# Five kinds of POOL work moved to ACT, DVE, transfers and a sum from PSUM, in a fused attention and routed transformer block with hand-written order lists

## The chip, the cores and the metric

The kernel runs on one core of a Trainium2 chip. The metric is the device time of one execution in microseconds (us), median of the runs shown; lower is better. A core has TensorE (PE, with its weight loads shown apart as PEld), VectorE (DVE), ScalarE (ACT), GpSimd (POOL) and SyncE (SP), which here issues every transfer. Each engine runs its own instructions in the order in which they were written and waits on semaphores.

## The reference, cut to what matters

Sixteen sequences of 512 tokens of width 128 go through two sublayers, each with a residual and a layer norm. All data are float32.

```python
# first sublayer: causal attention, 16 heads of 8
q, k, v = heads(x @ w_q.T), heads(x @ w_k.T), heads(x @ w_v.T)
q, k = rms_norm(q), rms_norm(k)
scores = tanh(q @ k.T / sqrt(8) / 50) * 50          # causal mask
x = layernorm(x + merge(softmax(scores) @ v) @ w_o.T)
# second sublayer: 63 tokens of each sequence are selected and processed
weights = x @ router_w + router_b
thr = top_k(weights, 64)[-1];  sel = the 63 tokens above thr
xs = x[sel];  hn = rmsnorm(xs, ln1)
o = attention(rope(hn @ wq), rope(hn @ wk), hn @ wv, mask[sel][:, sel]) @ wo
x1 = xs + o
x2 = x1 + gelu(rmsnorm(x1, ln2) @ w1) @ w2          # tanh form of gelu
out = scatter(x2 * weights[sel]) + x * (1 - selected)
x = layernorm(x + out)
```

## The kernel before, in words

**Pairs and stages.** The 16 sequences ("batches") make 8 pairs. `iterations(body)` (L474) writes the program out for p from -1 to 10, and in one iteration the stages of up to four pairs are in work: the first attention of pair p with the preparation of the next batch; `fin` and `route` and `sel` of pair p-1 (end of the first sublayer, router weights and ranks, gathering of the selected tokens, their q, k and v); `att` and `late` of pair p-2 (second attention, MLP, scatter, last layer norm); and `late` of pair p-3. Iterations 8 to 10 have no first attention left: they are the run-out of the last pairs.

**The main stream.** An iteration has 16 steps s, eight groups of heads for each of the two batches. For a group PE multiplies q and k into `ps_s` in two units (L1170, one step ahead of ACT), ACT takes tanh of each unit (L708) and, one step later, exp of the group (L723), POOL multiplies the diagonal blocks with a triangle (L619), and PE multiplies the result with v into `ps_y` (L1187, `pv.0` to `pv.7` of each batch).

**The order lists.** Everything else is "side work". `PE_ORDER`, `VE_ORDER`, `POOL_ORDER` and `ACT_ORDER` (L107 to L182) say for each of the 16 steps, in two halves, which side step an engine executes there, for which unit: `att.S0@-2` is step `att.S0` of pair p-2, `prep.qk1/0@1` is batch 0 of pair p+1. `run_side` (L479) writes them out. On DVE, which has side work alone, only the sequence counts. An engine waits at a step until its inputs are there, and everything behind it in its list waits too. Side steps of PE share two PSUM banks, "a" and "m"; `BANK` and `BANK_READ` say which bank a step writes and which earlier readers it must wait for.

**SP's queue** (L496 to L566) is in order as well. In iteration p it issues: `load_x`, `turn` of batch 1 of this pair (two transposing transfers of q and k from `st`, after POOL's `lo`), `load_res`, `load_x`, the two stores of pair p-3, `load_res`, `turn` of batch 0 of the next pair.

**The POOL work that the change touches.**
- `prep_sq` (L623): squares of q and k of a batch, 1024 columns, into `qk2`; DVE's `prep_ss` (L840) sums them, and the chain goes on through `root`, `prep_qkn`, `prep_split` (`hi`), POOL's `prep_lo` (L629) and `turn` to the scores of the batch.
- `route_xw` (L636): the normed tokens `x1` times the router's row into `r1`; DVE's `route_w` (L915) sums over 128 columns and adds the bias `rb`.
- `sel_zb` (L640): `z_base = x1 * coef`, 512 columns for each batch; DVE's `late_sc` (L1097) adds it to the scattered sum that PE left in PSUM. `fin_x1` (L905) may overwrite `x1` only after it.
- `att_kw` (L648): the 16 heads' keys spread into the block form `k_wide`, two multiplications of 1024 columns with the mask `head_of`. It waits for DVE's copy `sel.qkT` (L1017), and PE's `att_scores` (L1329, steps S0 and S1) waits for it.
- `att_hh` and `att_hu` (L656, L661): two of the products of the gelu. The chain is `att.h` on DVE (L1079), `hh` on POOL, `hp` on DVE (L1083), `hu` on POOL, tanh on ACT (L692), `att.g` on DVE (L1087), then `late.w2` on PE. ACT executes the tanh between the tanh and exp of its main stream.

Of the kernel before, what the change touches and what calls it, by code (L numbers as in the profile page):

```python
# [61 lines left out]
def moments_of(tiles, tag=""):  # L62
# [34 lines left out]
    "prep": ["sq", "lo_q", "lo_k"],  # L97
    "route": ["xw"],
    "sel": ["zb0", "zb1"],
    "att": ["kw0", "kw1", "hh", "hu"],  # L100
# [7 lines left out]
    ["sel.msel@-2", "att.S0@-2"], ["att.S1@-2"],  # L108
    ["pv.4/1@-1", "pv.5/1@-1"], ["pv.6/1@-1", "route.thr/1@-2", "pv.7/1@-1", "prep.qk0/1@0"],
    [], ["prep.qk1/1@0", "att.P0@-2"],  # L110
    ["att.P1@-2", "prep.v/1@0"], ["att.PV@-2"],
    [], ["prep.xT/0@1", "pv.0/0@0", "pv.1/0@0"],
    ["route.wrow/0@-1", "pv.2/0@0", "att.oT@-2"], ["pv.3/0@0"],
    ["fin.wo/1@-1", "att.wo@-2"], ["route.won/0@-1", "prep.qk0/0@1"],
    [], [],
    ["att.h2T@-2"], ["att.w1@-2", "prep.qk1/0@1", "pv.4/0@0"],
    ["pv.5/0@0", "route.wrow/1@-1"], ["pv.6/0@0", "pv.7/0@0"],
    ["route.thr/0@-1"], ["late.w2@-2", "prep.v/0@1"],
    ["route.won/1@-1"], ["sel.gather@-1", "sel.gather1@-1", "late.sc0@-2"],
    ["late.sc1@-2"], ["fin.wo/0@0", "pv.0/1@0"],  # L120
    ["pv.1/1@0", "pv.2/1@0"], ["sel.hnT@-1", "sel.ET@-1", "sel.qkv@-1", "pv.3/1@0"],
    ["sel.R@-1", "sel.qkT@-1"], ["sel.R1@-1", "sel.R2@-1", "sel.R3@-1"],
# [5 lines left out]
    ["route.coef/1@-2", "att.den@-2"],
    ["prep.qk0/1@0", "fin.yU1/1@-1", "prep.qk1/1@0"], ["att.PT0@-2"],
    ["att.PT1@-2", "prep.v/1@0", "prep.ss/1@0", "prep.root1/1@0"], ["prep.root2/1@0", "route.w/0@-1", "prep.qkn/1@0"],  # L130
    ["prep.hi/1@0"], ["prep.xT/0@1", "fin.y/1@-1", "route.row/0@-1", "att.o@-2", "fin.yT/1@-1"],
    ["att.oT@-2"], ["route.win/0@-1", "fin.res/1@-1", "att.x1f@-2", "fin.ln/1@-1", "att.ss@-2", "fin.root1/1@-1"],
    ["att.root1@-2", "route.rank/0@-1"], ["prep.qk0/0@1", "att.root2@-2", "att.hn@-2", "fin.root2/1@-1"],
    ["att.h2T@-2", "fin.x1/1@-1", "fin.yU0/0@0"], ["att.h@-2", "late.root2@-3", "att.hp@-2"],
    ["prep.qk1/0@1", "route.w/1@-1"], ["late.norm@-3", "att.g@-2", "route.row/1@-1", "route.win/1@-1"],
    [], ["route.coef/0@-1", "fin.yU1/0@0", "late.proc@-2", "prep.v/0@1", "route.rank/1@-1"],
    ["prep.ss/0@1", "fin.y/0@0"], [],
    ["sel.xs@-1", "sel.ss@-1", "prep.root1/0@1"], ["sel.root1@-1", "fin.yT/0@0"],
    ["late.z0@-2"], ["prep.root2/0@1"],
    ["sel.root2@-1"], ["prep.qkn/0@1", "sel.hn@-1", "prep.hi/0@1", "fin.res/0@0", "late.z1@-2"],  # L140
    ["sel.hnT@-1", "sel.ET@-1"], ["sel.qkv@-1"],
    ["late.ln@-2"], ["fin.ln/0@0", "sel.qkT@-1", "sel.R@-1"],
    ["prep.xT/1@1", "sel.RT@-1"], ["fin.yU0/1@0", "sel.msel@-1", "fin.root1/0@0", "att.sc0@-1"],
# [83 lines left out]
    "att.P0": ["att.sc0@0", "prep.qk0/1@2"],  # L227
    "att.P1": ["prep.qk1/1@2", "route.thr/1@0"],
    "att.PV": ["att.PT0@0", "prep.vb/1@2"],
    "att.S0": ["prep.xT/1@2", "sel.qkT@0"],  # L230
    "att.S1": ["sel.msel@0"],
    "att.h2T": ["att.x1f@0", "route.rank/0@1"],
# [5 lines left out]
    "late.sc0": ["late.x2@0", "route.rank/1@1"],
    "late.sc1": ["att.h@0", "sel.xs@1"],
    "late.w2": ["att.h2T@0", "route.row/1@1"],  # L240
    "prep.qk0/0": ["fin.res/1@-2", "prep.xT/0@0"],
# [5 lines left out]
    "prep.xT/0": ["att.PT1@-3", "prep.qk1/1@-1"],
    "prep.xT/1": ["fin.res/0@-1", "prep.qk1/0@0", "sel.qkT@-2"],
    "route.thr/0": ["att.h@-1", "prep.qk0/0@2"],
    "route.thr/1": ["att.sc1@0"],  # L250
    "route.won/0": ["att.x1f@-1", "prep.vb/1@1"],
    "route.won/1": ["late.x2@-1", "route.row/1@0"],
    "route.wrow/0": ["att.PT1@-1", "prep.xT/0@2"],
    "route.wrow/1": ["att.h2T@-1", "prep.qk1/0@2"],
    "sel.ET": ["late.z1@-1", "sel.xs@0"],
    "sel.R": ["sel.ET@0"],
    "sel.RT": ["sel.R@0"],
# [1181 lines left out]
```

## Time and profile before

| | |
|---|---|
| three runs | 791.93, 792.43, 793.32 us; median 792.43 |
| the profiled execution | 795.73 us |
| its span, first to last instruction | 793.9 us |
| mean granted TensorE clock | 0.821 of full speed |
| busy, share of the span | PE 82%, DVE 75%, ACT 70%, POOL 49% |
| one pair in the steady middle (365.93 to 447.83 us) | 81.90 us |
| the run-out after ACT's main stream (695 to 793.9 us) | 98.9 us |

The page of the profile gives the busy time of each engine, the chain of work that ended last and the costliest groups of instructions. Views of the trace then cut this by stretches of time, by line, by what an engine waited for, and by single instructions. A group of instructions shows count, busy time, mean duration in ns, and the idle time of the engine just before them with what ended it.

### The profile page before, as it was taken

The numbers are of one execution on the slowest core, as the hardware profiler recorded it, in microseconds if no ns is written. First come the engines' busy times: TensorE is split into PE (matmuls) and PEld (weight loads), VectorE is DVE, ScalarE is ACT, GpSimd is POOL, SyncE is SP. The second block draws the span as 40 slices with busy tenths as digits, with TensorE's granted clock in tenths as the row PEclk, the third lists the DMA queues.
The fourth block names the chain that finished last, engine by engine and source line by source line (L and its number), as shares of the span: only waits on it lengthen the run. The fifth ranks groups of instructions, "written<-read, shape, count | busy, mean of one in ns | idle before, by whom it ended". The sixth has DMA issues, their size and how long they took to land.

```text
span 793.9 us, 16532 instructions
## 1 busy us (share of the span) xinstructions
PE 650.0 (82%) x6384; PEld 373.9 (47%) x6384; DVE 596.5 (75%) x1649; ACT 553.3 (70%) x403; POOL 386.2 (49%) x399
## 2 busy tenths in 40 slices
PE   3387777889989998999989998999899979855742
PEld 2243323455546454555546454545464546344432
DVE  3651636765897889888988898788998887687656
ACT  0399887786988798879788978788798969500000
POOL 5244545536555475556646564556547653511210
PEclk9558667778989998899889988898999878965755
DMA  6303030405230323040412121030303040000001
GB/s 199 67 2 80 12 69 1 81 2 107 81 80 2 69 66 82 28 67 15 66 44 53 30 53 55 19 64 4 64 28 68 2 68 28 14 1 28 0 1 53
DMA packets 97855, 36.72 MB, mean 46 GB/s; under 512 B 69090, under 2 KB 95090, under 8 KB 97778
## 3 DMA queue, kind: packets, MB, share of 16 engines
q1 hardware_dynamic: 97778, 35.67, 20.4%
q8 instruction: 51, 0.84, 0.4%
q14 instruction: 26, 0.21, 0.1%
HBM read 14.69 MB, written 4.19 MB: 24 GB/s over the span
## 4 chain that ended last, share of the span: by engine, by line
PE 45%; DVE 27%; ACT 12%; issue 9%; POOL 4%; DMA 2%; SPq 1%; DVEq 0%; ACTq 0%; POOLq 0%
PE ps_y L1187 15%; PE ps_s L1170 10%; ACT pr L723 8%; ACT th L708 4%; PE ps_m L1286 3%; DVE wins L934 2%; POOL pr L619 2%; DVE qn_v L842 2%; PE ps_m L1371 1%; PE ps_a L1236 1%; PE ps_a L1218 1%; DVE v_aug L836 1%; DMA k_st<-st 1%; PE ps_m L1270 1%; PE ps_m L1194 1%
## 5 line engine op out<-in xcount | busy, mean ns | idle before, releaser
L708 ACT ACTIVATE th<-ps_s 128x1024 f32<-128x1024 f32 (+1 forms) x256 | 278.6, 1129 | 77.1 <-PE ps_s L1170 67.5
L619 POOL TENSOR_TENSOR pr<-pr,tri 128x320 f32<-128x320 f32 (+1 forms) x256 | 188.2, 757 | 192.9 <-ACT pr L723 192.8
L723 ACT ACTIVATE pr<-th 128x2304 f32<-128x2304 f32 x128 | 271.5, 2122 | 8.7 <-PE ps_y L1187 8.4
L1170 PE MATMUL ps_s<-q_st,k_st 32*64 32x512 f16 (+7 forms) x2048 | 190.8, 315 | 42.5 <-ACT th L708 34.6
L1187 PE MATMUL ps_y<-pr,v_aug 128*32 128x512 f32 (+7 forms) x2048 | 171.6, 469 | 7.8 <-POOL pr L619 7.6
L1170 PEld LDWEIGHTS ps_s<-q_st,k_st 32*64 32x64 f16 x2048 | 92.1, 114 | 168.0 <-issue 63.5
L633 POOL TENSOR_TENSOR st<-qk,st 128x1024 f16<-128x1024 f32 x32 | 76.7, 2417 | 49.5 <-DVE st L852 49.5
L1187 PEld LDWEIGHTS ps_y<-pr,v_aug 128*32 128x32 f32 x2048 | 58.3, 116 | 76.7 <-issue 47.6
L621 POOL TENSOR_TENSOR k_wide<-qkT,head_of 128x1024 f32<-128x1024 f32 x16 | 30.1, 1901 | 41.6 <-DVE qkT L1017 41.6
L694 ACT ACTIVATE sc<-hu 128x512 f32<-128x512 f32 x8 | 5.0, 630 | 64.3 <-POOL hu L621 64.3
L934 DVE SCALAR_TENSOR_TENSOR wins<-w_wide,x,later 128x512 f16<-128x512 f32 (+1 forms) x64 | 41.2, 644 | 2.6
L690 ACT ACTIVATE pm<-pm 128x1008 f32<-128x1008 f32 x8 | 8.3, 1043 | 41.9 <-DVE pm L1031 41.9
L621 POOL TENSOR_TENSOR z_base<-x,coef 128x512 f32<-128x512 f32 x16 | 17.1, 1067 | 41.4 <-DVE coef L958 41.4
L621 POOL TENSOR_TENSOR r<-x,rw_row 128x512 f32<-128x512 f32 x16 | 18.9, 1181 | 35.5 <-DVE x L910 35.5
L621 POOL TENSOR_TENSOR st<-qk 128x1024 f32<-128x1024 f32 x16 | 30.3, 1893 | 5.9 <-DVE qk L825 5.7
L825 DVE COPY qk<-ps_a 128x512 f32<-128x512 f32 x16 | 10.7, 666 | 28.9 <-PE ps_a L1218 28.9
L1286 PE MATMUL ps_m<-mask_a,E 128*64 128x512 f32 x112 | 31.0, 605 | 0.0
L1348 PE MATMUL ps_a<-vv,k_wide 128*128 128x32 f32 x128 | 19.7, 315 | 9.2 <-DVE v_aug L836 5.7
L860 DVE STREAM_TRANSPOSE y_u<-ps_y 128x512 f32<-128x512 f32 x32 | 22.6, 705 | 5.8 <-PE ps_y L1187 5.8
L1218 PE MATMUL ps_a<-wT,xT 128*128 128x256 f32 x64 | 25.1, 532 | 0.0
L1348 PEld LDWEIGHTS ps_a<-vv,k_wide 128*128 128x128 f32 x128 | 18.9, 234 | 11.1 <-issue 6.9
L825 DVE COPY qk<-ps_m 128x512 f32<-128x512 f32 x16 | 11.1, 691 | 14.7 <-PE ps_m L1218 14.6
(224 smaller groups left out, 1074.0 us busy)
## 6 DMA issues: line engine op xcount, KB each, us to landing
x_in<-in_L_attn_x SPq DMA_DIRECT2D x16, 256.0 KB, 3.5
...
q_st<-st SPq DMA_TRANSPOSE x16, 4.5
k_st<-st SPq DMA_TRANSPOSE x16, 4.8
```

Of the source, the lines that this page charges most:

```text
L619: return nc.gpsimd.tensor_tensor(buf, buf, tri[:, None, :].to_broadcast([P, blocks, 64]), ALU.mult)
L621: mul = lambda out, a, b: nc.gpsimd.tensor_tensor(out, a, b, ALU.mult)
L633: pl["prep"].done(nc.gpsimd.tensor_tensor(lo_parts[s], qk_twice[s], hi_parts[s], ALU.subtract), f"lo_{part}", b)
L708: nc.scalar.activation(th[:, gi % 2, c0:c1], ps_s[:, c0:c1], ACT.Tanh, scale=1.0 / (QK_SCALE ** 2 * DH ** 0.5 * SOFTCAP))\
L723: nc.scalar.activation(pr[:, probs_at(n):probs_at(n) + GROUP], th[:, gi % 2, :], ACT.Exp, scale=SOFTCAP).then_inc(exp_done, 1)
L860: ve["fin"].done(nc.vector.transpose(y_u[:, half], ps_y[:, :]), f"yU{half}", b)
L934: step(lambda: nc.vector.scalar_tensor_tensor(won[c], w_wide[:, P * c:], x1[:, k, c, D:D + 1], later[:, 0:n], ALU.is_le, ALU.mult, accum_o ...
L1170: last = mm(ps_s[64 * s:64 * s + 64, COL[kb]:COL[kb] + S - 64 * kb], k_st[rows, k, gi // 2, 64 * kb:64 * kb + 64], q_st[rows, k, gi // 2, ...
L1187: last = mm(ps_y[32 * j:32 * j + 32, 64 * kb:S], v_aug[:, k, kb, gi, :], pr[:, c:c + S - 64 * kb], start=(kb == 0), stop=(kb == NB - 1), s ...
L1218: last = mm(at(f"prep.qk{i}", b)[:, :].rearrange("p (n t e) -> p n t e", t=2, e=32)[:, :, t % 2], xT[:, P * t:P * t + P], wT[:, 0:2, :].re ...
L1286: last = mm(at("sel.R")[SLOTS * k:SLOTS * k + SLOTS, :], E[:, c, SLOTS * k:SLOTS * k + SLOTS], (mask_b if k and q < 2 else mask_a)[:, c, : ...
L1348: last = mm(at("att.PV")[:, 32 * n:32 * n + 32], PT[:, n, :], vv[:, n, :, :].rearrange("p k c -> p (k c)"), start=True, stop=True)
```

## The change

Five kinds of work leave POOL, which keeps the triangle and `prep.lo`:

- `prep.sq` becomes an ACT instruction, Square of 1024 columns. ACT's one Sin instruction of the setup moves behind the first of them.
- `hh` becomes an ACT Square of 512 columns (`att.sq`), `hp` and `hu` become one DVE instruction (`att.u`); a constant is drawn out into the scale of the tanh.
- `route.xw` and the two DVE instructions of `route.w` become four DVE instructions of 129 columns that multiply and sum (the bias is a 129th column, with ones in `x1`).
- `z_base` goes: `late_sc` multiplies and adds from PSUM in four instructions of 128 columns. `x1` and `coef` get a second buffer.
- `att_kw` goes: SP issues 16 transfers per pair (`widen`), one for each head, 8 partitions by 2 x 64 floats, into a `k_wide` that is zeroed once. They stand in SP's queue behind `turn` of batch 0 of the next pair. `PT`, which lay in `k_wide`, now lies in `hb` and `RT`.

The order lists and the bank tables are new throughout. In the new `ACT_ORDER`, step 2 has `att.exp@-2` and `prep.sq/1@0`, step 9 `att.sq@-2`, step 10 `att.tanh@-2` and `prep.sq/0@1`; in the new `POOL_ORDER`, step 4 has `prep.lo/1@0` and step 12 `prep.lo/0@1`, the steps at which they stood before. The core of the diff (in it, `prep_sq` and `att_sq` are ACT's, the loops over `c` DVE's `route_w` and `late_sc`, `att_scores` PE's):

```diff
-    "route": ["w", "w_b", "row", ...
+    "route": ["w0", "w1", "w2", "w", "row", ...
...
+PE_ORDER = (
+    ["att.S0@-2", "sel.msel@-2"], ["prep.qk0/1@0", "att.S1@-2", "pv.4/1@-1"],
+    ["prep.qk1/1@0"], ["route.thr/1@-2", "pv.5/1@-1", "pv.6/1@-1", "pv.7/1@-1"],
+    ["prep.v/1@0"], ["att.P0@-2"],
...
+    ["pv.0/1@0", "pv.1/1@0", "pv.2/1@0", "sel.hnT@-1"], ["sel.qkv@-1", "pv.3/1@0", "sel.R@-1"],
+    [], ["sel.qkT@-1", "sel.R1@-1", "sel.R2@-1", "sel.R3@-1", "prep.xT/1@1"],
+    [], ["sel.RT@-1"],
+)
+VE_ORDER = (
+    ["att.mx0@-2", "fin.root2/0@-1", "att.sc1@-2"], ["prep.qk0/1@0", "att.mx1@-2", "prep.qk1/1@0", "fin.x1/0@-1"],
+    ["route.w/0@-1", "route.coef/1@-2", "att.den@-2"], ["prep.v/1@0"],
...
+    ["att.hn@-2", "route.rank/0@-1", "att.h2T@-2"], ["late.norm@-3", "fin.root2/1@-1", "att.h@-2", "fin.x1/1@-1"],
+    ["route.w/1@-1", "prep.qk1/0@1", "att.u@-2", "route.row/1@-1"], ["route.win/1@-1", "route.coef/0@-1"],
...
+    ["sel.hn@-1", "prep.hi/0@1", "sel.ET@-1", "sel.hnT@-1"], ["late.z1@-2", "sel.qkv@-1", "late.ln@-2", "sel.qkT@-1"],
+    ["fin.ln/0@0", "sel.R@-1", "prep.xT/1@1"], ["fin.yU0/1@0", "sel.RT@-1", "late.root1@-2"],
+    ["fin.root1/0@0", "late.root2@-2"], ["sel.msel@-1", "att.sc0@-1"],
+)
...
-        x1 = sb("x1", [P, 2, NT, D + 1])
+        x1 = sb("x1", [P, 2, 2, NT, D + 2])
...
-        PT = k_wide[:, 0].rearrange("p h s -> p (h s)").rearrange("p (n c) -> p n c", n=H // 2)
+        PT = [hb[:, :].rearrange("p (n c) -> p n c", n=H // 4), RT]
...
+            def widen(q):
+                ve["sel"].wait(sp, q, "qkT")
+                pe["att"].wait(sp, q - 1, "S1")
+                if q == 0:
+                    sp.wait_ge(k_wide_zero, 1)
+                for h in range(H):
+                    rows = slice(DH * h, DH * h + DH)
+                    sp.dma_start(k_wide[rows, :, h, :], qkT[rows, 1, :].rearrange("p (k s) -> p k s", k=2))\
+                        .then_inc(keys_wide, 16)
...
                 if live(p + 1, PAIRS):
                     turn(Batch(p, 2), 0)
+                if live(p - 1, PAIRS):
+                    widen(p - 1)
...
+            def prep_sq(b, k):
+                ve["prep"].wait(act, b, "qk1")
+                if b.at_least(1):
+                    act.wait_ge(turned[1 - k], (b - 1).pair * 32 + 32)
+                nc.scalar.activation(qk2, qk_flat, ACT.Square).then_inc(squared, 1)
+                if b.no == 0:
+                    act.wait_ge(setup_ve, SETUP_RED)
+                    nc.scalar.activation(turn[:, :, :, :], red[:, :, :, :], ACT.Sin).then_inc(setup_act, 1)
...
+            def att_sq(q, _):
+                ve["att"].wait(act, q, "h")
+                nc.scalar.activation(hq[:, :], hb[:, :], ACT.Square).then_inc(square_ready, 1)
...
+                for c in range(NT):
+                    step(lambda: nc.vector.tensor_tensor_reduce(
+                        r1x[:, (D + 1) * c:(D + 1) * (c + 1)], x1[:, b.pair % 2, k, c, 0:D + 1], rw_row[:, :], 1.0, 0.0, ALU.mult, ALU.add,
+                        x1[:, b.pair % 2, k, c, D + 1:D + 2]), f"w{c}" if c < NT - 1 else "w")
...
+            def att_u(q, _):
+                v.wait_ge(square_ready, q + 1)
+                pe["late"].wait(v, q - 1, "w2")
+                ve["att"].done(nc.vector.scalar_tensor_tensor(hu[:, :], hq[:, :], 1.0 / 0.044715, hb[:, :], ALU.add, ALU.mult),
+                               "u", q)
...
-                pl["sel"].wait(v, q, f"zb{k}")
+                ve["route"].wait(v, Batch(q, k), "coef")
...
+                for c in range(NT):
+                    ve["late"].done(nc.vector.scalar_tensor_tensor(
+                        y_out[:, k, c], x1[:, q % 2, k, c, 0:D], coef[:, q % 2, k, c:c + 1],
+                        at(f"late.sc{k}")[:, P * c:P * c + P], ALU.mult, ALU.add), f"z{k}_{c}" if c < NT - 1 else f"z{k}", q)
...
             def att_scores(q, h):
-                pl["att"].wait(t_, q, "kw1")
+                t_.wait_ge(keys_wide, 16 * H * (q + 1))
```

## Rows read from the trace of the kernel before

**Rows 1.** The page: busy time by engine, and the chain that ended last

```profile
PE 650.0 (82%) x6384; PEld 373.9 (47%) x6384; DVE 596.5 (75%) x1649; ACT 553.3 (70%) x403; POOL 386.2 (49%) x399
...
PE 45%; DVE 27%; ACT 12%; issue 9%; POOL 4%; DMA 2%; SPq 1%; DVEq 0%; ACTq 0%; POOLq 0%
```

**Rows 2.** Stretches: length, busy PE, PEld, DVE, ACT, POOL, clock, DMA share, GB/s

```profile
365.93:447.83 81.90, 76.10 (x801) 43.79 (x805) 71.82 (x204) 68.61 (x51) 47.05 (x47) 0.90 0.23 46
695.00:793.90 98.90, 50.68 (x286) 39.29 (x282) 65.39 (x220) 3.34 (x4) 13.76 (x11) 0.60 0.06 17
```

**Rows 3.** Waits of ACT in that steady pair: us in total, times, longest

```profile
ACT th L708 <- PE ps_s L1170: 8.4, 6, 2.2
ACT sc L694 <- POOL hu L621: 3.5, 1, 3.5
```

**Rows 4.** Groups by line on POOL, whole run: the work that leaves it

```profile
L621 POOL TENSOR_TENSOR st<-qk 128x1024 f32<-128x1024 f32 x16 | 30.3, 1893 | 5.9 <-DVE qk L825 5.7
L621 POOL TENSOR_TENSOR k_wide<-qkT,head_of 128x1024 f32<-128x1024 f32 x16 | 30.1, 1901 | 41.6 <-DVE qkT L1017 41.6
L621 POOL TENSOR_TENSOR r<-x,rw_row 128x512 f32<-128x512 f32 x16 | 18.9, 1181 | 35.5 <-DVE x L910 35.5
L621 POOL TENSOR_TENSOR hu<-sc,hb 128x512 f32<-128x512 f32 x8 | 10.1, 1267 | 6.7 <-DVE sc L1083 6.7
```

**Rows 5.** Groups by line on DVE: what goes, and the nearest to what comes

```profile
L918 DVE TENSOR_REDUCE x<-r 128x4 f32<-128x512 f32 x16 | 10.8, 678 | 0.0
...
L919 DVE TENSOR_SCALAR x<-x,rb 128x4 f32<-128x4 f32 x16 | 5.4, 339 | 0.6
...
L1083 DVE TENSOR_SCALAR sc<-sc 128x512 f32<-128x512 f32 x8 | 3.4, 421 | 1.4 <-POOL sc L621 1.4
...
L1102 DVE TENSOR_TENSOR y_out<-ps_m,z_base 128x512 f32<-128x512 f32 x8 | 5.5, 683 | 0.3 <-PE ps_m L1387 0.3
...
L982 DVE CUSTOM_DVE_ANT_0 hn<-xs 128x128 f32<-128x128 f32 x8 | 3.0, 377 | 0.3
...
L1093 DVE SCALAR_TENSOR_TENSOR x<-ps_a,x1f 128x128 f32<-128x128 f32 x8 | 2.3, 286 | 3.0 <-PE ps_a L1378 3.0
...
L1087 DVE SCALAR_TENSOR_TENSOR hu<-sc,hb 128x512 f32<-128x512 f32 x8 | 5.5, 683 | 0.6 <-ACT sc L694 0.6
```

**Rows 6.** Single instructions of DVE and POOL around 405 us: start, duration

```profile
405.39 0.96 DVE L804 SCALAR_TENSOR_TENSOR lo_v<-lo_v 128x8 f32<-128x8 f32 x1
...
406.59 0.17 DVE L806 SCALAR_TENSOR_TENSOR lo_v<-lo_v 128x8 f32<-128x8 f32 x1
...
405.30 1.03 POOL L621 TENSOR_TENSOR sc<-hb 128x512 f32<-128x512 f32 x1
```

**Rows 7.** Groups by line on ACT, whole run: the side work that it has

```profile
L690 ACT ACTIVATE pm<-pm 128x1008 f32<-128x1008 f32 x8 | 8.3, 1043 | 41.9 <-DVE pm L1031 41.9
...
L694 ACT ACTIVATE sc<-hu 128x512 f32<-128x512 f32 x8 | 5.0, 630 | 64.3 <-POOL hu L621 64.3
```

**Rows 8.** SP's queue at the start, transfers one behind another: start, duration

```profile
2.20 2.63 SPq L504 DMA_DIRECT2D pr<-in_L_attn_w_o  x4
...
8.04 0.43 SPq L511 DMA_DIRECT2D w_sb<-in_L_ffn_w  x1
8.51 0.43 SPq L512 DMA_DIRECT2D w_sb<-in_L_ffn_w  x1
...
9.54 0.33 SPq L514 DMA_DIRECT2D rb_one<-in_L_ffn_router_b  x1
9.91 0.36 SPq L515 DMA_DIRECT2D g<-in_L_ffn_ln  x1
```

**Rows 9.** Transfers: issuing line, count, size, median us from issue to landing

```profile
pr<-in_L_attn_w_v SPq DMA_DIRECT2D x1, 64.0 KB, 1.8
```

**Rows 10.** The keys on their way at the end of the steady pair: start, duration

```profile
439.76 0.42 DVE L1017 COPY qkT<-ps_a 128x256 f32<-128x256 f32 x1
...
440.26 1.90 POOL L621 TENSOR_TENSOR k_wide<-qkT,head_of 128x1024 f32<-128x1024 f32 x1 [3.40 <-DVE qkT L1017]
...
444.36 0.64 PE L1334 MATMUL ps_a<-k_wide,qkT 128*64 128x512 f32 x1
```

**Rows 11.** The gate of the last pair on DVE: start, duration

```profile
772.24 0.69 DVE L1079 COPY hb<-ps_m 128x512 f32<-128x512 f32 x1 [2.17 <-PE ps_m L1371]
...
777.77 0.68 DVE L1087 SCALAR_TENSOR_TENSOR hu<-sc,hb 128x512 f32<-128x512 f32 x1
```

More of the change, by code:

```diff
@@ L96 @@
 POOL_STEPS = {
[L97 to L100, printed above, removed]
+    "prep": ["lo_q", "lo_k"],
 }
 PE_ORDER = (
[L108 to L122, printed above, removed]
@@ L128 @@
[L128 to L140, printed above, removed]
@@ L141 @@
[L141 to L143 removed]
+    ["att.mx0@-2", "fin.root2/0@-1", "att.sc1@-2"], ["prep.qk0/1@0", "att.mx1@-2", "prep.qk1/1@0", "fin.x1/0@-1"],
+    ["route.w/0@-1", "route.coef/1@-2", "att.den@-2"], ["prep.v/1@0"],
+    [], ["att.PT0@-2", "prep.ss/1@0"],
+    ["prep.xT/0@1", "att.PT1@-2", "fin.yU1/1@-1"], ["prep.root1/1@0", "prep.root2/1@0"],
@@ L174 @@
     [], [],
-    [], ["att.tanh@-2"],
     [], [],
+    [], ["prep.lo/0@1"],
+    [], [],
+    [], [],
+    [], [],
+)
+ACT_ORDER = (
+    [], [],
+    [], [],
+    ["att.exp@-2"], ["prep.sq/1@0"],
+    [], [],
+    [], [],
+    [], [],
+    [], [],
+    [], [],
+    [], [],
+    ["att.sq@-2"], [],
+    ["att.tanh@-2"], ["prep.sq/0@1"],
     [], [],
@@ L226 @@
 BANK_READ = {
[L227 to L232, printed above, removed]
+    "att.P0": ["route.thr/1@0"],
+    "att.P1": ["att.sc1@0", "prep.vb/1@2"],
+    "att.PV": ["att.PT0@0", "prep.xT/0@3"],
+    "att.S0": ["sel.R@0"],
+    "att.S1": ["att.sc0@0"],
+    "att.h2T": ["att.PT1@0", "route.rank/0@1"],
@@ L233 @@
     "att.oT": ["att.o1@0"],
-    "att.w1": ["att.PT1@0", "fin.res/1@1", "prep.qk0/0@3"],
+    "att.w1": ["att.x1f@0", "prep.qk0/0@3"],
     "att.wo": ["att.oT@0"],
-    "fin.wo/0": ["late.z0@-2", "prep.qk1/0@1", "route.rank/1@-1"],
+    "fin.wo/0": ["prep.qk1/0@1", "sel.xs@-1"],
     "fin.wo/1": ["route.row/0@0"],
[L238 to L241, printed above, removed]
@@ L242 @@
-    "prep.qk0/1": ["att.sc0@-2", "prep.xT/1@0"],
+    "late.sc0": ["late.x2@0"],
+    "late.sc1": ["att.h2T@0", "fin.res/0@2", "sel.xs@1"],
+    "late.w2": ["att.h@0", "route.rank/1@1"],
+    "prep.qk0/0": ["att.x1f@-3", "prep.xT/0@0"],
+    "prep.qk0/1": ["prep.xT/1@0", "sel.msel@-2"],
     "prep.qk1/0": ["att.h2T@-3", "prep.vb/1@-1", "route.rank/0@-2"],
-    "prep.qk1/1": ["prep.vb/0@0", "route.thr/1@-2"],
+    "prep.qk1/1": ["att.sc1@-2", "fin.res/0@-1", "prep.qk1/0@0"],
     "prep.v/0": ["prep.qk0/0@0", "route.thr/0@-2"],
-    "prep.v/1": ["att.PT0@-2", "prep.qk0/1@0"],
@@ L247 @@
[L247 to L257, printed above, removed]
@@ L258 @@
-    "sel.gather": ["prep.vb/0@2", "route.thr/0@0"],
-    "sel.hnT": ["fin.res/0@1", "late.z0@-1"],
+    "prep.v/1": ["prep.qk1/1@0"],
+    "prep.xT/0": ["att.PT0@-3", "prep.qk0/1@-1"],
+    "prep.xT/1": ["prep.vb/0@0", "sel.qkT@-2"],
+    "route.thr/0": ["route.row/1@0"],
+    "route.thr/1": ["prep.qk0/1@2", "sel.msel@0"],
+    "route.won/0": ["fin.res/1@0"],
+    "route.won/1": ["prep.vb/0@2", "route.thr/0@0"],
+    "route.wrow/0": ["att.PT1@-1", "prep.vb/1@1"],
+    "route.wrow/1": ["att.h@-1", "prep.qk0/0@2"],
@@ L260 @@
+    "sel.ET": ["late.z0@-1", "route.rank/1@0"],
+    "sel.R": ["fin.res/0@1", "late.z1@-1"],
+    "sel.RT": ["prep.xT/1@2", "sel.qkT@0"],
+    "sel.gather": ["att.h2T@-1", "prep.qk1/0@2"],
+    "sel.hnT": ["sel.ET@0"],
     "sel.msel": ["sel.RT@0"],
@@ L634, in prep_lo @@
                                     f"lo_{part}", b)
[L636 to L667 removed]
+            table = {"prep.lo": prep_lo}
             def body(p):
```

207 lines of the change are left out of this document (85 added, 122 removed), and 3 rows, old and new, of the table VE_STEPS.

## The prediction, made before the changed kernel was run

> **What bounds the kernel now.** I read the page's busy times and chain first [rows 1]. PE has 45% of the chain, DVE 27%, ACT 12%, POOL 4%: what POOL does is seldom what the end waits for. Busy shares of the whole span mix two states, so I cut the span into stretches next [rows 2]. In a steady pair of 81.90 us PE is busy for 76.10, DVE for 71.82, ACT for 68.61, POOL for 47.05: three engines are nearly full, and none of them is POOL. In the run-out, 98.9 us after ACT's main stream, nothing is full, and the time is the length of one dependent chain. Third I read what ACT, which paces the groups, waits for in the steady pair [rows 3]: 8.4 us for PE's scores and 3.5 us for the gelu's `hu` from POOL. So POOL reaches the time in three places: that wait, the hold that it puts on single DVE instructions, and its links in the run-out.
>
> **DVE.** Per pair two sums of 0.678, two additions of 0.339, `hp` of 0.421 and two last sums of 0.683 go: 3.82 us. Eight multiply-and-sums (nearest row: the fused square and sum, 0.377), eight 128-column instructions from PSUM (0.286) and `att.u` (as `att.g`, 0.683) come: 5.99 us [rows 5]. That is +2.2 us on an engine with 10.1 us free in a pair. Against it, a removed POOL instruction can free DVE: beside `hh` an instruction of 8 columns took 0.96 us, its like 0.17 us [rows 6], 0.8 us in a pair. Bounds of the relief: 0, and 0.8 for each of the ten POOL instructions that leave a pair, 8 us; I take 0.8, the one case that the row shows. The Trainium skill ("SBUF — State Buffer", SBUF: two separate sides) says that GpSimd and DVE share a pair of ports under an exclusive lock, held for a whole instruction, and that the loser blocks; the row agrees, 0.96 us beside POOL's 1.03 us. Net DVE: **+1.4 us**.
>
> **ACT.** Two Squares of 1024 columns and one of 512 come. By the side work that ACT has now, 1.043 us for 1008 columns and 0.630 us for 512 [rows 7], that is 2.7 us a pair, 71.3 of 81.9: it fits beside the rest. Each is also a new wait: ACT stands at `prep.sq` for DVE's `qk1`, at `att.sq` for `att.h`, at the tanh for `att.u`, with the tanh and exp of the next group behind it, and PE's scores behind those. I cost these waits at nothing as long as DVE keeps its place in the lists; without that cover each costs what DVE is late. In return the wait of 3.5 us [rows 3] goes, because POOL's 1.0 and 1.27 us [rows 4, 6] and a DVE step leave the gate's chain. DVE, fuller than ACT, stays short, so I count two thirds of it, **-2.3 us** (bounds 0 and -3.5).
>
> **The keys.** Now DVE ends the copy of `qkT` at 440.18, POOL spreads it in two instructions of 1.9 us, and PE starts S0 at 444.36, 4.2 us after the copy [rows 10]. Afterwards SP issues 16 transfers. No row shows one of 8 partitions; the starts of neighbours lie 0.37 us apart behind a transfer of a single number, 0.47 behind one of the large weights, and 0.66 in a piecewise one (2.63 for four) [rows 8]; a 64 KB transfer lands 1.8 us after its issue [rows 9]. With 0.42, the middle of the two plain ones, the last lands 15 x 0.42 + 1.8 = 8.1 us after the first issue, so S0 starts some **4.0 us later** than now. Bounds: all 16 at once, 1.8 us, S0 could be 2.4 us earlier; at 0.66, 11.7 us, 7.5 us later. SP itself is free then, as `lo/0` keeps its step and `turn` is out before the copy; behind the 16 stand only `load_x` and the `turn` of the next iteration, a quarter pair away, which I cost at nothing. PE's S0 has `msel`, the second unit of scores and `qk0/1` queued behind it, and DVE's `msel` and `sc0` wait for both. What covers it is the work between: on PE the mask rows, `xT`, scores and `RT`; on DVE `fin.ln`, four copies and two roots. It is of the length of the present 4.2 us, not of 8. I take 2.4 us a pair (bounds 0 and 4.0 at this spacing).
>
> Two rules meet here. The rows say that each transfer holds SP's queue for 0.33 to 0.66 us, a fifth to a third of its landing time. The Trainium skill ("DMA: Bandwidth & Descriptors", Issuing engines are not separate DMA queues) calls the time that initiating a transfer takes usually small beside the transfer itself; no run here shows 16 small ones in a row. By that rule S0 would not wait at all; it is a rival below.
>
> **Edits at nothing.** The second buffer of `x1` and `coef` only takes waits away; PE's gather gets one column more of 129; `PT` in `hb` and `RT`, last read half a pair before; the memset of `k_wide` on POOL, which is idle then. The new lists add no instruction, but they decide how DVE's free 10.1 us are spent: a gain cannot exceed those, a loss may be as large. With no row for it I take 0 and keep a quarter, 2.5 us a pair either way, for the range.
>
> **Sum.** A steady pair: +1.4 - 2.3 + 2.4 = +1.5 us; six iterations have the whole mix, +9. In the first two pairs only the first attention is in work, so ACT is likelier the chain and its four Squares of 1.04 us may count in full, 4.2, or not at all; half, +2.1. Run-out: the last pair has nothing beside its chain, so the later S0 counts in full, +4.0; in the iteration before, `pv.4` of the last batch stands behind S0 in PE's list, +3.0 of 4.0. The gate shrinks: now 4.84 us from the end of `att.h` (772.93) to `att.g` (777.77) [rows 11], afterwards 0.63 + 0.68 + 0.63 [rows 5, 7] and, estimated, 0.3 of hand-overs, -2.6. The last sums: 4 x 0.286 for 0.683, twice, +0.9. Together +5.3. In all 9 + 2.1 + 5.3 = **+16.4 us**. The durations are of the profiled execution, 795.73 us with a span of 793.9, 3.3 above the median of the three runs; as I only add differences, they go onto the median: 792.4 + 16.4 = **809 us**, slower by 2%.
>
> **Rivals.**
> *Freed DVE (faster).* POOL holds DVE far oftener than the one row that I counted. Place: the ten POOL instructions that leave a pair; price 0.8 us each. It decides from four of them on: relief 3.2 instead of 0.8, the whole 3.5 at the gate, and S0 still 2.4 late make +2.2 - 3.2 - 3.5 + 2.4 = -2.1 a pair, -13; with +1 left of the start and run-out, **780**. For it: DVE is nearly full, so every microsecond counts. Against it: only one such instruction of this size lies in the steady pair that I read, and the triangle, POOL's most frequent work, stays.
> *Short issue (faster).* SP hands the 16 over quickly, S0 does not wait: +1.4 - 2.3 = -0.9 a pair, -5; run-out 5.3 - 7.0 - 2.4 = -4; start +2: **785**. This is what the page's rule gives. Against it: no issue in the rows takes under 0.33 us [rows 8].
> *Full wait (slower).* S0's 4.0 us count in every pair, and the gate gives nothing, because ACT now stands at `att.sq` instead: +1.4 + 4.0 = 5.4 a pair, 32; run-out +6, start +2: **832**. For it: PE and DVE both stand still at one place, and ACT runs dry behind them.
> *No effect.* POOL is 4% of the chain; what comes and goes cancels: **792**.
>
> **Numbers.** Forecast 0.42, full wait 0.21, freed DVE 0.20, short issue 0.10, no effect 0.07. Slower: 0.42 + 0.21 = 0.63; faster 0.30; within 0.2%, 1.6 us, about what a measurement of this kernel can tell from no change, 0.07. The range takes in the list's 2.5 us x 6 about the forecast (794 to 824), the full wait above and the freed DVE below: 779 to 832. The slower cases alone reach from 795 to 832.
>
> **What would show it.** Right: SP's queue with 16 issues 0.35 to 0.5 us apart behind each `qkT`; S0 about 8 us after the copy, with PE idle before it for a transfer into `k_wide`; a steady pair of 83 to 84 us with DVE busy for 73; ACT's wait for `hu` gone; POOL under 36 us a pair (47.05 less four groups, 89.4 us over eight pairs, [rows 4]); the run-out longer by about 5. Wrong: issues under 0.15 us apart, or S0 no later than 4.2 us after the copy; a pair under 81 us with DVE busy under 71 (freed DVE); ACT waiting more than 2 us a pair for `att.h` or `qk1` (full wait).

## The result, and the profile after

The changed kernel takes **870.55 us** (median of four runs, 869.25 to 872.85) against 792.18 for the kernel before beside it: a ratio of 1.100, with an interval of 1.0955 to 1.1052. The forecast was 809, so the sign was right, but of 78 us more only 16 were forecast. The profiled execution took 871.44 us, with a span of 869.6.

The page of the changed kernel: busy time by engine, and the chain that ended last.

```profile
PE 666.3 (77%) x6384; PEld 390.1 (45%) x6384; DVE 608.5 (70%) x1793; ACT 575.6 (66%) x428; POOL 282.6 (33%) x318
...
PE 40%; DVE 22%; ACT 14%; SPq 11%; issue 9%; DMA 2%; POOL 2%; DVEq 0%; ACTq 0%
```

The new transfers, by their line: shortest, median and longest issue in ns, first and last start.

```profile
L551 SPq DMA_DIRECT2D k_wide<-qkT x128: 685/686/860, 185.9 to 824.4; - x128
```

POOL lost 104 us of work, as the change meant it to. But SP's queue, 1% of the chain before [rows 1], is now 11% of it, 10% by the line of the 16 transfers of a pair, of 0.69 us each. The same steady pair as in [rows 2] (the fifth; length, busy PE, PEld, DVE, ACT, POOL, clock):

```profile
392.10:485.10 93.00, 79.36 (x796) 46.87 (x795) 73.97 (x223) 71.42 (x55) 33.97 (x36) 0.84 0.22 42
```

The long exp of ACT's main stream, by its line (first and last start):

```profile
L705 ACT ACTIVATE pr<-th x128: 2107/2124/2132, 38.8 to 743.8; 128x2304 f32<-128x2304 f32 x128
```

A steady pair has grown from 81.90 to 93.00 us. What follows the last exp has grown too: 125.8 us now, 107.3 before (that exp started at 686.6 of 793.9). The waits of that pair (us in total, times, longest):

```profile
ACT th L690 <- PE ps_s L1162: 28.0, 12, 9.1
DVE msel L1002 <- PE ps_a L1310: 9.7, 1, 9.7
...
PE ps_m L1326 <- DMA k_wide<-qkT: 8.1, 1, 8.1
```

PE, DVE and ACT all stand still at one place, and it is the same one: S0, in all eight pairs. It waits for the keys. The place in single instructions (start, duration):

```profile
466.16 0.42 DVE L1003 COPY qkT<-ps_a 128x256 f32<-128x256 f32 x1
466.60 11.65 SPq L551 DMA_DIRECT2D k_wide<-qkT  x16
...
479.37 1.98 PE L1326 MATMUL ps_m<-k_wide,qkT 128*64 128x512 f32 x4 [8.13 <-DMA k_wide<-qkT]
...
482.72 0.22 DVE L1002 COPY msel<-ps_a 128x64 f32<-128x64 f32 x1 [9.72 <-PE ps_a L1310]
483.93 1.24 ACT L690 ACTIVATE th<-ps_s 128x1280 f32<-128x1280 f32 x1 [9.11 <-PE ps_s L1162]
485.82 1.98 PE L1326 MATMUL ps_m<-k_wide,qkT 128*64 128x512 f32 x4
```

S0 starts 12.8 us after the end of the copy, against 4.2 before [rows 10]. There is a second loss in these rows: the four matmuls of S0, and those of S1 6 us later, take 1.98 us. In the kernel before, S1 took 1.08:

```profile
446.21 1.08 PE L1334 MATMUL ps_m<-k_wide,qkT 128*64 128x512 f32 x4
```

The stretches of the changed kernel around them (length, busy PE, PEld, DVE, ACT, POOL, granted clock) show why:

```profile
470.00:473.00 3.00, 1.24 (x12) 0.64 (x10) 2.41 (x12) 3.00 (x3) 0.42 (x1) 1.00 0.03 6
473.00:476.00 3.00, 0.00 (x0) 0.00 (x0) 0.01 (x1) 1.73 (x2) 1.41 (x2) 0.87 0.03 6
476.00:479.00 3.00, 0.00 (x0) 0.00 (x0) 0.00 (x0) 0.00 (x0) 0.00 (x0) 0.50 0.03 7
479.00:482.00 3.00, 2.63 (x16) 1.39 (x17) 0.00 (x0) 0.00 (x0) 0.00 (x0) 0.50 0.32 93
...
485.00:488.00 3.00, 3.00 (x11) 0.67 (x13) 0.88 (x6) 2.18 (x2) 0.74 (x1) 0.50 0.00 0
488.00:491.00 3.00, 3.00 (x20) 1.05 (x14) 2.42 (x5) 1.02 (x1) 0.67 (x2) 0.85 0.00 0
```

PE stands idle from 471.2 to 479.4, its clock falls from 1.00 to 0.50, the lower of its levels (1.2 GHz), and stays there for some 10 us after work has begun again. This wait of PE is paid twice.

### The profile page after: what moved, and what is told of

It reads as the page before. It is cut to its first block, busy times and chain, and to the rows that moved or that the text cites. A ratio compares the mean times of both kernels' runs of the same rounds, so it can differ in the third digit from the quotient of the medians.

```text
span 869.6 us, 16752 instructions
## 1 busy us (share of the span) xinstructions
PE 666.3 (77%) x6384; PEld 390.1 (45%) x6384; DVE 608.5 (70%) x1793; ACT 575.6 (66%) x428; POOL 282.6 (33%) x318
## 4 chain that ended last, share of the span: by engine, by line
PE 40%; DVE 22%; ACT 14%; SPq 11%; issue 9%; DMA 2%; POOL 2%; DVEq 0%; ACTq 0%
PE ps_y L1179 12%; SPq L551 10%; PE ps_s L1162 9%; ACT pr L705 8%; ACT th L690 5%; PE ps_a L1340 3%; PE ps_m L1326 3%; DVE y_out L1105 2%; DMA k_wide<-qkT 2%; PE ps_m L1210 2%; DVE stats L863 1%; PE ps_a L1210 1%; PE ps_a L1310 1%; DVE v_aug L818 1%; SPq L535 1%
## 5 line engine op out<-in xcount | busy, mean ns | idle before, releaser
L628 POOL TENSOR_TENSOR pr<-pr,tri 128x320 f32<-128x320 f32 (+1 forms) x256 | 195.9, 787 | 424.4 <-ACT pr L705 424.4
L1162 PE MATMUL ps_s<-q_st,k_st 32*64 32x320 f16 (+7 forms) x2048 | 193.3, 324 | 54.9 <-ACT th L690 50.7
L1179 PE MATMUL ps_y<-pr,v_aug 128*32 128x512 f32 (+7 forms) x2048 | 158.0, 453 | 1.1 <-POOL pr L628 1.1
L1326 PE MATMUL ps_m<-k_wide,qkT 128*64 128x512 f32 x64 | 26.2, 910 | 72.5 <-DMA k_wide<-qkT 70.1
L919 DVE SCALAR_TENSOR_TENSOR wins<-w_wide,x,later 128x512 f16<-128x512 f32 (+1 forms) x64 | 53.2, 831 | 2.9
L1326 PEld LDWEIGHTS ps_m<-k_wide,qkT 128*64 128x64 f32 x64 | 4.2, 179 | 77.5 <-DMA k_wide<-qkT 72.2
L672 ACT ACTIVATE sc<-hb 128x512 f32<-128x512 f32 x8 | 5.0, 631 | 42.4 <-DVE hb L1067 42.3
L661 ACT ACTIVATE st<-qk 128x1024 f32<-128x1024 f32 x16 | 16.8, 1048 | 13.3 <-DVE qk L807 13.3
L1210 PE MATMUL ps_m<-wT,xT 128*128 128x256 f32 x64 | 25.2, 535 | 0.0
L834 DVE CAST st<-qk 128x1024 f16<-128x1024 f32 x32 | 25.0, 821 | 0.1
```

Source lines behind the costliest of these rows:

```text
L628: return nc.gpsimd.tensor_tensor(buf, buf, tri[:, None, :].to_broadcast([P, blocks, 64]), ALU.mult)
L919: step(lambda: nc.vector.scalar_tensor_tensor(won[c], w_wide[:, P * c:], x1[:, b.pair % 2, k, c, D + 1:D + 2], later[:, 0:n], ALU.is_le, A ...
L1162: last = mm(ps_s[64 * s:64 * s + 64, COL[kb]:COL[kb] + S - 64 * kb], k_st[rows, k, gi // 2, 64 * kb:64 * kb + 64], q_st[rows, k, gi // 2, ...
L1179: last = mm(ps_y[32 * j:32 * j + 32, 64 * kb:S], v_aug[:, k, kb, gi, :], pr[:, c:c + S - 64 * kb], start=(kb == 0), stop=(kb == NB - 1), s ...
L1210: last = mm(at(f"prep.qk{i}", b)[:, :].rearrange("p (n t e) -> p n t e", t=2, e=32)[:, :, t % 2], xT[:, P * t:P * t + P], wT[:, 0:2, :].re ...
L1326: last = mm(at(f"att.S{h}")[rows, :], qkT[:, 0, rows], k_wide[:, k, 8 * h:8 * h + 8, :].rearrange("p h s -> p (h s)"), start=True, stop=True)
```

## The experiments

Each kernel ran beside the kernel before (medians of 791.5 to 793.4 us).

### Is it the transfers, and what do they cost?

**e1_keys_on_pool** undoes one part: POOL spreads the keys again.

```diff
-  widen(p - 1)                             # SP: 16 transfers
+  pl["att"].done(mul(k_wide[:, k], qkT[...], head_of[...]), f"kw{k}", q)   # POOL, twice
```

> The changed kernel with one part undone: the keys are spread by POOL's two multiplications again, right after the copy of qkT, and SP issues no transfers for them; everything else is as changed. Theory A (the 16 issues are the whole loss): the eight waits of PE's S0 for the transfers, 70 us together, go; S0 starts about 4 us after the copy; 785 to 800 us. Theory B (the Squares on ACT, the longer DVE work and the new lists cost as well): 815 to 840 us, with ACT waiting for att.h, att.u or qk1 by more than 2 us a pair.

**e2_widen_alone** makes this part alone, in the kernel before.

> The kernel before with one part of the change alone: the keys are spread by SP's 16 transfers, under the old lists (PT lies in hb and RT, as it must); nothing else. Theory A: the 16 issues take 0.73 us each here too, S0 starts 13 us after the copy instead of 4.2, and the pairs grow by about 9 us: 850 to 870 us. Theory C (the new lists put S0 where nothing covers it, the old ones don't): under 820 us.

**e3_half_of_heads** and **e9_two_heads** issue fewer transfers and leave out the keys of the other heads.

```diff
-  for h in range(H):
+  for h in range(H // 2):      # e9: range(2)
       sp.dma_start(k_wide[rows, :, h, :], qkT[rows, 1, :]...)
```

> The changed kernel with 8 transfers instead of 16: the heads 8 to 15 are left out of k_wide, which stays zero there. If each transfer costs SP 0.73 us in a row, S0 starts 5.8 us earlier in each of eight pairs: 870 - 47 = 823 us (815 to 830), the issues of a group end after 5.8 us. If the 11.7 us are a fixed price of the group, or S0 waits for something else, 860 to 870 us.

> The changed kernel with 2 transfers instead of 16: the heads 2 to 15 are left out of k_wide, which stays zero there, so that neither SP's queue nor POOL has work worth naming for the keys. Theory R (S0's wait counts one for one and the rest of the change is about neutral): from 16 to 8 transfers S0's wait fell by 47 us over eight pairs and the time by 51; the 23 us of wait that are left at 8 go too, 794 to 800 us. Theory W (the added work costs 20 us by itself, as keys on POOL at 817 us seemed to say): 812 to 819 us.

**e4_one_piece_per_row** changes the layout of `k_wide`, so that a partition receives 128 numbers in one piece.

```diff
-  k_wide = sb("k_wide", [P, 2, H, SLOTS])
+  k_wide = sb("k_wide", [P, H, 2 * SLOTS])
```

> The changed kernel with k_wide laid out so that a transfer writes one piece of 128 numbers per partition instead of two of 64: 16 transfers of the same bytes with half the pieces. If the issue is paid per transfer, 0.73 us each as now and 870 us. If it is paid per piece, about 0.37 us each, S0 5.8 us earlier, 823 us.

Measured: e1 **816.96** us (1.0346, 1.0264 to 1.0428); e2 **890.64** (1.1275, 1.1201 to 1.1348); e3 **819.40** (1.0375, 1.0307 to 1.0443); e4 **864.26** (1.0940, 1.0868 to 1.1011); e9 **781.81** (0.9849, 0.9822 to 0.9875).

The count decides: 16, 8 and 2 transfers give 870.6, 819.4 and 781.8 us. With two of them the changed kernel is *faster* than the kernel before, so the keys carry the whole loss, 89 us, and the rest of the change is worth 11 us at most, as e9 also spares the spreading of fourteen heads. e2 came out above both of its theories: under the old lists the transfers cost 98 us, so it is not the new lists that leave them uncovered. What an issue costs, from e3 (one group of eight) and e4 (ns: shortest, median, longest):

```profile
448.94 5.82 SPq L551 DMA_DIRECT2D k_wide<-qkT  x8
```

```profile
L551 SPq DMA_DIRECT2D k_wide<-qkT x128: 624/624/1442, 184.6 to 815.3; - x128
```

Eight take half of the time of sixteen, so nothing in it is fixed for the group. Half the pieces at the same bytes take 624 instead of 686 ns, 9% less: most of the price is paid per transfer. The spacing is 0.73 us. The Trainium skill ("DMA: Bandwidth & Descriptors", Issuing engines are not separate DMA queues) calls the time of initiating a transfer usually small beside the transfer; here an issue takes 0.69 us, the last one ends at 478.25, and S0 starts 1.1 us after that, so the rows disagree with it.

The same pair in e9, and its ACT waits:

```profile
358.90:440.60 81.70, 75.89 (x801) 45.22 (x801) 73.94 (x222) 71.14 (x54) 34.58 (x36) 0.90 0.24 47
```

```profile
ACT th L690 <- PE ps_s L1162: 8.4, 7, 3.1
...
ACT sc L672 <- DVE hb L1067: 0.9, 1, 0.9
```

Against it, the 93.00 us of the changed kernel are 11.3 us more: 7.8 in which PE is idle (93.00 - 79.36 against 81.70 - 75.89) and 3.5 in which PE is busy with the same work at a lower clock (0.84, not 0.90). After the last long exp (675.8 in e9) 104.3 us are left, 21.5 fewer than the changed kernel's 125.8.

But e1 fits neither theory: without any transfer it is still 24 us slower than before, in B's range, yet B's sign isn't there (in the pair from 460.8 us ACT waits for `att.h` for 0.7 us). Something else happens when POOL has the keys.

### Undoing other parts under lists made for them

> The kernel e1_keys_on_pool (changed kernel, keys by POOL, 817 us) with the two Squares of the norm a pair back on POOL, as multiplications right behind qk1. Theory W (added work on ACT counts in full, since ACT and PE take turns at one buffer of scores and ACT has no time of its own): 16 Squares of 1.05 us are 17 us, 800 us (797 to 804). Theory L (the new lists make the scores late): 812 to 820 us.

> The kernel e1_keys_on_pool with the gelu's chain back on POOL (hh and hu by POOL, hp by DVE, no Square on ACT). Theory W: ACT loses 0.63 us a pair, 5 us, but stands for hu again as it did before the change (3.5 us in the pair that was read): 815 to 835 us. Theory L: 812 to 820 us.

> The kernel e1_keys_on_pool (new work of ACT and DVE, keys by POOL) under the order lists and bank tables of the kernel before, the Squares put in behind their inputs. Theory W: ACT's 2.7 us a pair are there as well, 812 to 822 us. Theory L: the lists were the loss, 790 to 800 us.

> The kernel e1_keys_on_pool with both undone: the norm's Squares and the gelu's chain are POOL's again, so that ACT has the work it had before; what is left of the change are the lists, the weighted sums of the router on DVE and the last sums from PSUM. Theory W: 793 to 803 us. Theory L: 812 to 820 us.

Their edit is one of place: `prep.sq`, `att.hh` and `att.hu` go back into POOL's list behind their inputs, `att.hp` into DVE's, a few entries behind the place of `att.u`; e7 takes the lists and bank tables of the kernel before. Measured: e5 **851.77**, e6 **887.28**, e7 **877.05**, e8 **884.27** us. Both theories fall for e1's loss. Taking work off ACT made e1 slower by 35 to 70 us, and the old lists made the new work slower by 60. These four don't price the parts: the steps that I put back stand at places of my own choice. In e6 ACT waits for `hu` for 79.0 us over eight pairs, in the kernel before for 64.3. What they show is only that the same work, at another place or under other lists, took 35 to 70 us more; through which waits was not followed further.

### Why the keys cost elsewhere

**e10_keys_half** halves POOL's part, with a whole output: S0 needs only partitions 0 to 63 and S1 the others, so the keys are spread over 8 places instead of 16. **e11_before_keys_half** does the same in the kernel before.

```diff
-  k_wide = sb("k_wide", [P, 2, H, SLOTS])
+  k_wide = sb("k_wide", [P, 2, H // 2, SLOTS])      # one multiplication
...
-  mm(S[rows, :], qkT[:, 0, rows], k_wide[:, k, 8 * h:8 * h + 8, :])
+  mm(S[rows, :], qkT[64 * h:64 * h + 64, 0, rows], k_wide[64 * h:64 * h + 64, k, :, :])
```

> The kernel e1_keys_on_pool (changed kernel, keys by POOL, 817 us) with the keys spread over 8 places instead of 16, so that POOL multiplies once, 1024 numbers a partition instead of twice, and S0 and S1 each contract over their own 64 partitions; the output is whole. Theory H (in keys on POOL the multiplications hold DVE, whose copy of R before the RT transposes is late by 3 us in each pair): about half of it goes, 802 to 809 us. Theory W: 814 to 818 us, as ACT and DVE have the same work.

> The kernel before with the same halved spreading of the keys and nothing else, under the old lists: POOL has 15 us less to do and S0 can start 1.9 us earlier in each pair. If the keys are on the path of the old kernel too: 778 to 786 us. If the old lists cover them: 790 to 794 us.

Measured: e10 **827.55** us (1.0447, 1.0387 to 1.0507), slower than e1 with half of the work; e11 **795.28** (1.0023, 0.9982 to 1.0065), no difference: under the old lists the keys on POOL are covered. A later pair of e10, first in single instructions, then in stretches (length, busy PE, clock):

```profile
538.01 1.90 POOL L625 TENSOR_TENSOR k_wide<-qkT,head_in 128x1024 f32<-128x1024 f32 x1 [3.47 <-DVE qkT L1005]
538.75 1.19 DVE L868 TENSOR_TENSOR mv<-stats 128x4 f32<-128x4 f32 x1
...
542.05 0.68 DVE L965 COPY w_wide<-ps_m 128x512 f32<-128x512 f32 x1
...
543.43 1.09 PE L1188 MATMUL ps_a<-ident,w_wide 128*128 128x128 f32 x4 [1.89 <-DVE w_wide L965]
...
545.43 1.97 PE L1329 MATMUL ps_m<-k_wide,qkT 64*64 64x512 f32 x4
```

```profile
542.00:544.00 2.00, 0.57 (x3) 0.82 0.38 114
544.00:546.00 2.00, 2.00 (x11) 0.50 0.00 0
...
560.00:562.00 2.00, 2.00 (x15) 0.50 0.00 0
```

POOL's multiplication holds a DVE instruction of 4 columns for 1.19 us, its like takes 0.17. DVE copies R (`w_wide`) late, PE stands still for 1.9 us ahead of the RT transposes, and then works at the lower clock beyond 562. e1's gap at this place is longer, 2.90 us at 541.36, but only some 6 us at 0.50 follow it; so in the pairs around these two gaps PE is idle for 8.3 us in both kernels, and busy for 84.15 us in e10, 79.72 in e1. So the size of POOL's part isn't the point; the gap on PE and the clock behind it are. The next kernels test that.

```diff
 # e14: DVE's list at that place, keys by POOL as in e10
-["fin.ln/0@0", "sel.R@-1", "prep.xT/1@1"]
+["sel.R@-1", "fin.ln/0@0", "prep.xT/1@1"]
 # e12: DVE spreads the keys itself, straight from PSUM; e13: behind sel.R
+nc.vector.tensor_tensor(k_wide, t[:, P:2 * P]..., head_in..., ALU.mult)
 # e15 (as e12) and e16 (as e10)
+["sel.R@-1", "prep.xT/1@1", "fin.ln/0@0"]
 # e17 (three) and e18 (two): as e12; second unit of scores, last group of a second batch
-for kb in UNIT_BLOCKS[u]:
+for kb in UNIT_BLOCKS[u] * (3 if gi == 7 and k == 1 and u == 1 else 1):
```

> The changed kernel with the keys spread by DVE itself, halved (8 places, 1024 numbers a partition, one instruction, straight from PSUM beside the copy of the queries): no transfers, no POOL; the output is whole. Theory H (with keys on POOL the multiplication holds DVE ahead of the copy of R, PE stands still at the RT transposes and then runs at half clock): the hold is gone and DVE has 1.1 us more in a pair, 782 to 792 us. If keys on POOL cost for another reason, such as S0's later start: 805 us or more here too, since S0 can't start before DVE is done.

> The kernel e12_keys_on_dve with DVE's spreading of the keys behind the copy of R instead of ahead of the moments. Theory H: R is copied 1 us earlier than in e12, PE never stands still there, 781 to 791 us, and not above e12 by more than 2 us. Otherwise: 805 us or more.

> The kernel e10_keys_half (keys by POOL in one multiplication, 827.6 us) with one entry of DVE's list moved: the copy of R ahead of the moments of the first batch, so that what POOL holds is no longer ahead of it. Theory H: PE's idle time at the RT transposes (14 to 17 us over eight pairs) and the half clock behind it go, 785 to 800 us. If the hold isn't the cause: 820 to 830 us.

Measured: e12 **807.61** us (1.0165, 1.0118 to 1.0212), e13 **815.40** (1.0290, 1.0268 to 1.0312), e14 **839.54** (1.0605, 1.0577 to 1.0633). Theory H, in which the hold of DVE by POOL's keys is the cause, falls: e12 and e13 have no such multiplication, and keep the gap. (POOL still holds DVE in e12: beside the triangle, from 528.47 to 529.90, two instructions of the moments, of 4 columns each, take 0.71 and 0.51 us, their like 0.17. That is 0.9 us of a gap of 1.65.) The trace of e14 tells what stood there beside R; copy of xT, and the RT transposes:

```profile
555.18 0.69 DVE L804 COPY xT<-ps_a 128x512 f32<-128x512 f32 x1
...
555.97 1.09 PE L1188 MATMUL ps_a<-ident,w_wide 128*128 128x128 f32 x4 [2.21 <-issue]
```

RT goes into the bank in which xT lies, and the copy of xT still stood behind the moments: the gap was there as before, 2.2 us, with another step at its end. This tie is new: before the change RT went into bank "m" and waited for the copy of R alone. In e13 the keys stand between the copies of R and xT, so that they are ahead of RT again; why e13 lies above e12 stays open.

> The kernel e12_keys_on_dve (807.6 us, PE idle for 1.65 us ahead of the RT transposes in a later pair, then at half clock) with DVE's copies of R and xT ahead of the moments of the first batch. Theory G (that gap on PE and the half clock behind it are the loss): no gap above 1 us there, steady pairs of 81 to 83 us, 780 to 791 us in all. If not: 803 us or more.

> The kernel e10_keys_half (827.6 us, keys by POOL in one multiplication) with the same two copies ahead of the moments. Theory G: the gap of 1.9 us goes and with it most of the half clock, 783 to 800 us. If not: 820 to 840 us, as e14_r_ahead.

Measured: e15 **786.70** us (0.9913, 0.9881 to 0.9944) and e16 **807.52** (1.0176, 1.0131 to 1.0220). Moving the moments behind both copies is worth 21 us with the keys on DVE (e12 to e15) and 20 on POOL (e10 to e16); against e14, where only R is ahead, it is 32. PE's RT transposes of e15 no longer wait, and the sixth pair takes 83.70 us (length, busy PE, PEld, DVE, ACT, POOL, clock):

```profile
440.60:524.30 83.70, 77.21 (x799) 45.54 (x797) 74.24 (x223) 71.25 (x54) 33.98 (x36) 0.88 0.22 45
```

```profile
518.47 0.66 PE L1185 MATMUL ps_a<-ident,w_wide 128*128 128x128 f32 x4
```

e16 isn't all the way: in its later pairs gaps of 0.76 and 1.09 us stand ahead of the `msel` matmuls and of `prep.qk0`, and the clock falls again behind them (pairs of 89.6 us). That these are its remaining loss was not tried.

> The kernel e12_keys_on_dve (807.6 us) in which PE computes the second unit of scores of each second batch's last group three times instead of once, right ahead of the RT transposes: 20 useless matmuls, 1.4 us of PE in each of eight pairs, and ACT gets that unit so much later. Theory C (the lower clock behind the gap is what costs): PE has no gap above 0.5 us there, the half clock behind it goes, 788 to 800 us in spite of the added work. Theory G0 (the standing time itself costs): 807 to 816 us.

> The same with that unit computed twice, 0.7 us of the gap of 1.65 filled. Theory C: between e17_scores_thrice and e12_keys_on_dve, 790 to 806 us. Theory G0: 807 to 812 us.

Measured: e17 **787.34** us (0.9957, 0.9935 to 0.9980). Work that is of no use, 160 matmuls more, makes e12 20 us *faster*. In e18 the six runs lay between 788.4 and 821.5, median 812.3, so no ratio is given. Five of the six are above theory C's 806: half of the filling, which in the profiled run (821.5) left a gap of 1.31 us at 539.25 and some 17 us at 0.50 behind it, mostly doesn't help. The sixth pair as a stretch, in e12 and then in e17, is the one in which they differ most (the fourth is longer in e17, 87.7 against 83.5):

```profile
447.10:537.10 90.00, 82.92 (x798) 47.47 (x798) 75.92 (x223) 71.35 (x54) 34.41 (x36) 0.82 0.21 42
```

```profile
448.80:530.00 81.20, 75.39 (x823) 45.10 (x825) 74.84 (x224) 71.31 (x55) 34.61 (x36) 0.92 0.21 47
```

At its end, in single instructions of PE, the RT transposes, `prep.qk0` and S1, again of e12 and then of e17:

```profile
531.22 0.63 PE L1185 MATMUL ps_a<-ident,w_wide 128*128 128x128 f32 x4 [1.65 <-DVE w_wide L957]
...
535.87 2.07 PE L1209 MATMUL ps_a<-wT,xT 128*128 128x256 f32 x4
...
537.88 1.97 PE L1326 MATMUL ps_m<-k_wide,qkT 64*64 64x512 f32 x4
```

```profile
524.13 0.66 PE L1185 MATMUL ps_a<-ident,w_wide 128*128 128x128 f32 x4
...
527.88 1.13 PE L1209 MATMUL ps_a<-wT,xT 128*128 128x256 f32 x4
528.95 1.08 PE L1326 MATMUL ps_m<-k_wide,qkT 64*64 64x512 f32 x4
```

The added scores lie some 5 us ahead of the RT transposes, not right ahead of them as I had written; they make PE later by 1.1 us (2.26 us of scores instead of 1.17), and DVE's moments, now ahead of POOL's triangle, run without the hold. So when PE comes to RT the copy of R is done. Of the 8.8 us by which the pair is shorter, only 1.3 are less standing time. The rest is the clock: 0.92 over the pair instead of 0.82, and PE is busy for 75.39 us with *more* matmuls than took 82.92. The stretches around that place (length, busy PE, clock), of e12 and then e17:

```profile
529.00:532.00 3.00, 1.35 (x18) 1.00 0.29 87
532.00:535.00 3.00, 3.00 (x30) 0.78 0.00 0
535.00:538.00 3.00, 3.00 (x16) 0.50 0.00 0
538.00:541.00 3.00, 3.00 (x12) 0.50 0.00 0
```

```profile
522.00:525.00 3.00, 3.00 (x30) 1.00 0.20 60
525.00:528.00 3.00, 3.00 (x37) 1.00 0.09 28
```

The Trainium skill ("TensorE: Matmul & The Clock Gate", HAM oscillation — how this bites in real kernels) describes such a round: a wait in each pass lets the clock fall, and the next pass starts slow. The traces agree in kind, with 0.50 behind the gaps of the pairs shown. But what a gap costs is not fixed. In the same run of e12, the gap of 1.71 us at 357.08 was followed by 19 us at 1.00, and that of 1.70 us at 440.24 by some 17 us at 0.50 (an early and a later stretch of each; length, busy PE, clock):

```profile
356.00:358.00 2.00, 0.92 (x8) 1.00 0.28 83
...
366.00:368.00 2.00, 2.00 (x27) 1.00 0.00 0
```

```profile
442.00:444.00 2.00, 2.00 (x15) 0.50 0.04 8
...
456.00:458.00 2.00, 2.00 (x13) 0.50 0.00 0
```

What decides between them no run shows. Nor are the fast kernels free of it: in the steady pair of the kernel before, PE waits once for ACT's tanh ahead of its scores, and then works at 0.50 from about 401 to 407.

```profile
399.71 0.62 PE L1170 MATMUL ps_s<-q_st,k_st 32*64 32x512 f16 x6 [2.28 <-ACT th L708]
...
402.00:404.00 2.00, 2.00 (x12) 0.50 0.00 0
```

## Why the prediction was right or wrong

- **The keys: the failing term.** "With 0.42, the middle of the two plain ones": an issue measured 0.73 from start to start. The row that was nearest in kind, the piecewise transfer at 0.66 [rows 8], had been read as the far bound; the truth lay even above it. S0 came 12.8 us after the copy, not 8.2, which is 8.6 us later than before, not 4.0. With the next two terms this made 89 us of the keys (11.3 in each of six pairs and 21.5 at the end), where the sum had 21 (2.4 in each, and 7.0).
- **"I take 2.4 us a pair (bounds 0 and 4.0 at this spacing)."** The work named as cover stood ahead of S0 and was done at 471.2, 4.7 us after the copy, about as long as the 4.2 that the text gave it. So nothing was left to cover a later S0, and a discount of 1.6 us had no ground: PE waited 8.1 of the 8.6 us. And the bound itself was wrong in kind: against e9 a pair grew by 11.3 us, more than S0's delay, because a delay of PE was priced at its length, without the lower clock behind it. No step of the prediction priced the clock, though the 0.60 of the run-out stood in [rows 2].
- **The run-out.** Forecast +5.3, of it +7.0 for S0; measured +18.5, of it +21.5 for S0 (125.8 less 104.3): two groups of transfers, each with nothing beside it. The rest came out at -3.0 (104.3 less 107.3), forecast -1.7.
- **DVE.** +2.2 us came in full: 73.94 of a pair's time in e9 against 71.82. The relief of 0.8 doesn't show in it.
- **ACT and the gate: right.** Forecast +2.7 and a wait reduced by 2.3; measured +2.5 (71.14 against 68.61) and 2.6 (3.5 us for `hu` before [rows 3], 0.9 for `att.h` now). The Squares do fit beside the rest, and in that pair ACT does not wait for DVE by the more than 2 us that were the sign of the full wait.
- **The start.** Forecast +2.1. In e9 the 33rd long exp starts 157.4 us after the first, before 162.8 us: -5.4, with ACT's Squares and all.
- **The sum without the keys** was, by those terms, 6 x (1.4 - 2.3) + 2.1 - 1.7 = -5 us; measured -11. What the text said would be seen of these parts is there in the changed kernel as well: DVE busy for 73.97 of a pair (forecast 73), POOL for 33.97 (under 36).
- **The lists: "2.5 us a pair either way".** In the changed kernel itself they cost nothing that shows (e9 is 11 us faster than before). With the keys on POOL or DVE the band is too narrow for single entries: from e14 to e16 the place of one cost 32 us, 4 us in each of eight pairs.
- **The range** ended at the full wait, 832. That rival had the place right, but took 4.0 us; the bound of 7.5 us that the text itself worked out for a spacing of 0.66 was not carried into the range. In eight pairs it is 60 us, 852.
